# A two-layer decoder on one core: where the 16x16 inverses of the second self-attention run, and what stands between them

## The reference, cut to what matters

```python
A = jnp.tril(jnp.einsum('bhik,bhjk->bhij', K, K) * bt[:, :, None, :], -1)
Vn = jax.scipy.linalg.solve_triangular(eye + A, rhs, lower=True)   # rhs = V
scores = jnp.einsum('bqhd,bkhd->bhqk', q, k) * scale               # k times beta, causal mask
attn = jax.nn.softmax(scores, axis=-1)
out = jnp.einsum('bhqk,bkhd->bqhd', attn, v)                       # v is Vn
```

## Time and profile before

| what | us |
|---|---|
| median of three runs | 1125.17 (1124.74 to 1133.2) |
| the profiled execution, its own time | 1135.51 |
| its span, first to last instruction | 1133.7 |
| TensorE busy in the span | 989.1 |
| VectorE busy | 567.4 |
| ScalarE busy | 366.7 |
| GpSimd busy | 195.9 |

### The profile page before, as it was taken

One profiled execution on the slowest core, in us unless ns is written; L12 is line 12 of the kernel. 1 busy time (PEld: TensorE's weight loads), 2 busy tenths in 40 slices (PEclk: granted clock), 3 DMA queues, 4 the chain that ended last, 5 costly groups with the idle time before them and its releaser, 6 DMA issues.

```text
span 1133.7 us, 18852 instructions
## 1 busy us (share of the span) xinstructions
PE 989.1 (87%) x7392; PEld 619.5 (55%) x7392; DVE 567.4 (50%) x1153; ACT 366.7 (32%) x733; POOL 195.9 (17%) x233
## 2 busy tenths in 40 slices
PE   7998779998899999975863999889489999999994
PEld 4764423333468899962352568668345444444442
DVE  3789878885431111115687676356652333233325
ACT  4434436666222233322374453233221000000000
POOL 6000000000012222210036631060000111111110
PEclk9889869999799999986986999997679999999998
DMA  6000000000744555532001102030104022222001
GB/s 227 2 1 1 1 1 2 1 1 1 270 152 162 162 181 181 182 94 74 1 2 37 38 2 94 1 134 2 47 1 114 15 85 85 82 77 79 17 1 37
DMA packets 27209, 75.06 MB, mean 66 GB/s; under 512 B 9828, under 2 KB 17260, under 8 KB 21748
## 3 DMA queue, kind: packets, MB, share of 16 engines
q1 hardware_dynamic: 24916, 67.84, 18.1%
q0 software_dynamic: 2208, 6.03, 1.9%
HBM read 67.41 MB, written 6.46 MB: 65 GB/s over the span
## 4 chain that ended last, share of the span: by engine, by line
PE 71%; DVE 22%; issue 3%; ACT 2%; DMA 1%; POOL 0%; SPq 0%; DVEq 0%; ACTq 0%; POOLq 0%
PE psum L1519 8%; PE psum L1094 7%; PE psum L1106 7%; DVE arena L2073 4%; PE psum L1523 3%; PE psum L1285 3%; PE psum L1507 3%; PE psum L1549 2%; PE psum L1553 2%; PE psum L996 2%; PE psum L1485 2%; DVE arena L1996 2%; DVE arena L1997 2%; PE psum L1442 2%; PE psum L1255 1%
## 5 line engine op out<-in xcount | busy, mean ns | idle before, releaser
L1519 PE MATMUL psum<-arena 128*128 128x512 f32 (+1 forms) x192 | 92.0, 616 | 0.5 <-DVE arena L2500 0.5
L1950 ACT ACTIVATE arena<-psum 128x512 f32<-128x512 f32 (+1 forms) x32 | 19.0, 594 | 225.6 <-PE psum L1523 225.6
L2073 DVE TENSOR_REDUCE arena<-psum 128x2 f32<-128x512 f32 x128 | 82.7, 688 | 15.6 <-PE psum L942 13.4
L1770 ACT ACTIVATE arena<-psum,arena 128x128 f32<-128x128 f32 x184 | 52.6, 368 | 115.2 <-PE psum L1094 94.8
L1094 PE MATMUL psum<-arena 128*128 128x128 f32 x736 | 86.7, 276 | 0.0
L1094 PEld LDWEIGHTS psum<-arena 128*128 128x128 f32 x736 | 84.0, 192 | 2.7 <-issue 2.7
L736 POOL TENSOR_TENSOR arena<-arena 128x512 f32<-128x512 f32 (+1 forms) x32 | 40.5, 1265 | 254.6 <-ACT arena L1950 254.6
L1106 PE MATMUL psum<-arena 128*128 x368 | 83.1, 379 | 0.0
L2220 DVE COPY arena<-psum 128x256 f32<-128x256 f32 x23 | 9.8, 425 | 135.6 <-PE psum L1079 85.2
L1747 ACT ACTIVATE arena<-psum 128x1024 f32<-128x1024 f32 x64 | 65.5, 1025 | 33.9 <-PE psum L964 30.9
L1106 PEld LDWEIGHTS psum<-arena 128*128 128x128 f32 x368 | 68.2, 190 | 8.4
(11 more groups left out here) (354 smaller groups left out, 1867.8 us busy)
## 6 DMA issues: line engine op xcount, KB each, us to landing
arena<-in_w SPq DMA_DIRECT2D x31, 1024.0 KB, 13.4
arena<-in_experts SPq DMA_DIRECT2D x8, 1248.0 KB, 6.2
arena<-mixed SPq DMA_DIRECT2D x16, 256.0 KB
arena<-mixed SPq DMA_DIRECT2D x8, 512.0 KB
arena<-in_ctx SPq DMA_DIRECT2D x2, 1024.0 KB, 7.1
arena<-returned SPq DMA_DIRECT2D x8, 256.0 KB, 4.9
arena<-in_w_xattn SPq DMA_DIRECT2D x1, 1538.5 KB, 9.9
arena<-in_w_ffn SPq DMA_DIRECT2D x1, 1152.0 KB, 5.2
```

Source lines behind the costliest of these rows:

```text
L1519: pe.matmul(out, e[w][:, k, :], xe6[:, half, k, :], start=(k == 0), stop=False)
L1770: last = act.activation(hidt[:, r % 2, ic * P:(ic + 1) * P], bank(n)[:, i * P:(i + 1) * P], ACT.Gelu, bias=b1_tile[:, r % 4, ic:ic + 1])
L2073: ax_max.by(dve.tensor_reduce(nmx[:, b % 2, :, h], bank(u % 2).rearrange("p (t s) -> p t s", t=2), AX.X, ALU.max, negate=True))
```

## The change

- GpSimd inverts half 0, VectorE half 1. GpSimd's inverse is followed by `keys_by_head` for w = 3 and 4, then the unit copy, then w = 5 and later.
- The diagonal of half 0 is transposed within the loop of the key products: at j = 6, after the transposes of tile 6 and before the products of m = 5 (`DIAG_AFTER` = 4). Its four banks take places 20 to 23 in the turn of six banks, so later products move by four places (`slot1`, `before_slot`). ScalarE's four copies (`keep_diagonal(0)`) stand at the same place.
- For that, the gathers of half 0 come earlier: VectorE's two after the products of m = 3 at j = 5, and ScalarE's one becomes a GpSimd copy (`gather_pool`). `ti1` is blanked by halves, with 1 + 4 memsets each.
- VectorE waits for all eight diagonal copies, and inverts columns 0 to 3, 4 to 7, 8 to 11 and 12 to 14 with one softmax behind each group. `scores1(0)` no longer waits for the diagonal copies; the first rest product does.
- ScalarE's unit copies are cut in halves (`own_unit`) and set after the exponentials of w = 0 and 1, and into rounds t = 0 and 1 of the solve loop.
- `pt1` is used from its middle on (`probs1`), so that the first eight probabilities do not lie over `nd1` and `ti1`; the four buffers of `nd1` and `ti1` are split so that each can be written when the part of `qk1` under it has been read. SyncE's fetch of half 0 waits for half 0's transposes only.

```diff
@@ build: arena
 arena.at = first1_at
-nd1, ti1 = arena.take(2, CH, CHUNKS * CH), arena.take(2, CH, CHUNKS * CH)
+nd1_first, ti1_first, ti1_last, nd1_last = (arena.take(CH, CHUNKS * CH) for _ in range(4))
+nd1, ti1 = (nd1_first, nd1_last), (ti1_first, ti1_last)
...
@@ build: slots, invert1
 
-def invert1(engine, do, step, g):
-    less, inv = (v[:, g, :, :].rearrange("p j (c i) -> p j c i", c=CHUNKS) for v in (nd1, ti1))
-    for j in range(CH - 1):
+DIAG_AFTER = 4
+DIAG_SLOT = (4 * (DIAG_AFTER + 1), 4 * (NT + 1))
+
+def slot1(m, r):
+    return 4 * m + r + (CHUNKS if m > DIAG_AFTER else 0)
+
+def probs1(w):
+    return pt1[:, (w + NT) % (2 * NT), :]
+
+def invert1(engine, do, step, g, columns):
+    less, inv = (v[g].rearrange("p j (c i) -> p j c i", c=CHUNKS) for v in (nd1, ti1))
+    for j in columns:
...
@@ SyncE
 sp.wait_ge(ti1_ready[g].sem, 1)
-sp.dma_start(mine, ti1[:, g, :, :].rearrange("p j x -> p (j x)")).then_inc(ti1_out[g].sem, 16)
+sp.dma_start(mine, ti1[g].rearrange("p j x -> p (j x)")).then_inc(ti1_out[g].sem, 16)
...
 if g == 0:
-    sp.wait_ge(nd1_ps.sem, nd1_ps.base + 2 * CHUNKS)
+    sp.wait_ge(nd1_ps.sem, nd1_ps.base + CHUNKS)
...
@@ GpSimd
     keys_by_head(w)
-pool.wait_ge(tr1_ps.sem, 2 * NT)
-do(pool.memset(ti1.rearrange("p g j x -> p (g j x)"), 0.0))
-for m in range(CH):
-    pool.memset(ti1.rearrange("p g j (c i) -> p g j c i", c=CHUNKS)[:, :, m, :, m], 1.0)
+
+def unit_inverse(g):
+    flat = ti1[g].rearrange("p j x -> p (j x)")
+    do(pool.memset(flat, 0.0))
+    for c4 in range(CHUNKS):
+        pool.memset(flat[:, CH * c4:CH * c4 + (CH - 1) * (CHUNKS * CH + 1) + 1:CHUNKS * CH + 1], 1.0)
+
+pool.wait_ge(na_act.sem, na_act.base + 2 * 4)
+pool.wait_ge(na_dve.sem, na_dve.base + 2 * 4)
+pool.wait_ge(kb1_ready.sem, 3)
+do(pool.tensor_copy(na1[64:96, 0, 0:CH, :], na1[64:96, 2, 0:CH, :]), gather_pool)
+pool.wait_ge(tr1_ps.sem, 2 * 4)
+unit_inverse(0)
+pool.wait_ge(tr1_ps.sem, 2 * 6)
+unit_inverse(1)
...
                     c["ident"].rearrange("p (c w) -> p c w", c=CHUNKS)[:, :, 0:CH]), ti1_blank)
-pool.wait_ge(nd1_sb.sem, nd1_sb.base + 2 * CHUNKS)
-invert1(pool, do, pool_step, 1)
+pool.wait_ge(nd1_sb.sem, nd1_sb.base + CHUNKS)
+invert1(pool, do, pool_step, 0, range(CH - 1))
+for w in range(3, 5):
+    keys_by_head(w)
+pool.wait_ge(kb1_ready.sem, 5)
...
                     wide(c["ident"][96:P, 96:96 + CH], 1, B * KC * 8)), unit_pool)
-for w in range(3, 2 * NT):
+for w in range(5, 2 * NT):
...
@@ TensorE: before_slot, keys_by_keys
 
+def before_slot(n):
+    last = n - 6
+    if last < 0:
+        return
+    if DIAG_SLOT[0] <= last < DIAG_SLOT[0] + CHUNKS:
+        pe.wait_ge(nd1_sb.sem, nd1_sb.base + last - DIAG_SLOT[0] + 1)
+        return
+    m, r = divmod(last - (CHUNKS if last >= DIAG_SLOT[0] else 0), 4)
+    if r < 2:
+        pe.wait_ge(na_act.sem, na_act.base + 2 * m + r + 1)
+    else:
+        pe.wait_ge(na_dve.sem, na_dve.base + 2 * m + r - 1)
+
...
     for r in range(4):
-        n = 4 * m + r
-        if n >= 6:
-            m0, r0 = divmod(n - 6, 4)
-            if r0 < 2:
-                pe.wait_ge(na_act.sem, na_act.base + 2 * m0 + r0 + 1)
-            else:
-                pe.wait_ge(na_dve.sem, na_dve.base + 2 * m0 + r0 - 1)
+        before_slot(slot1(m, r))
...
             last = pe.matmul(
-                bank((4 * m + r) % 6).rearrange("p (c u e i) -> p c u e i", c=CHUNKS, u=4, e=2)[:, :, u, :, :],
+                bank(slot1(m, r) % 6).rearrange("p (c u e i) -> p c u e i", c=CHUNKS, u=4, e=2)[:, :, u, :, :],
...
@@ TensorE: turn_diagonal
 if g == 0:
-    pe.wait_ge(na_act.sem, na_act.base + 2 * NT)
-    pe.wait_ge(na_dve.sem, na_dve.base + 2 * NT)
-pe.wait_ge(gather_act.sem, gather_act.base + g + 1)
+    pe.wait_ge(gather_pool.sem, gather_pool.base + 1)
+else:
+    pe.wait_ge(gather_act.sem, gather_act.base + 1)
...
 for i in range(CH):
-    last = pe.transpose(bank(4 * g + i // 4)[:, (i % 4) * P:(i % 4 + 1) * P],
+    if i % 4 == 0:
+        before_slot(DIAG_SLOT[g] + i // 4)
+    last = pe.transpose(bank((DIAG_SLOT[g] + i // 4) % 6)[:, (i % 4) * P:(i % 4 + 1) * P],
...
@@ TensorE: the loop over tiles, scores1
         turn_heads1(j)
+    if j == DIAG_AFTER + 2:
+        turn_diagonal(0)
...
         keys_by_keys(j - 1)
-for g in range(2):
-    turn_diagonal(g)
+turn_diagonal(1)
...
         pe.wait_ge(causal_ready.sem, causal_ready.base + 1)
-        pe.wait_ge(nd1_sb.sem, nd1_sb.base + 2 * CHUNKS)
...
@@ TensorE: rest_of_chunk
 chunk, group = divmod(t, GROUPS)
+if t == 0:
+    pe.wait_ge(nd1_sb.sem, nd1_sb.base + 2 * CHUNKS)
...
     if chunk < 3:
-        pe.wait_ge(unit_act.sem, unit_act.base + chunk)
+        pe.wait_ge(unit_act.sem, unit_act.base + 2 * chunk)
...
@@ ScalarE: keep_products, gather
             na1[:, :, 4 * m:4 * m + 4, 32 * r:32 * r + 32],
-            bank((4 * m + r) % 6).rearrange("p (c u x) -> p c u x", c=CHUNKS, u=4), ACT.Copy))
-
-def gather(g):
-    act.wait_ge(na_act.sem, na_act.base + 2 * 4 * (g + 1))
-    act.wait_ge(na_dve.sem, na_dve.base + 2 * 4 * (g + 1))
-    gather_act.by(act.activation(na1[64:96, 0, g * CH:(g + 1) * CH, :], na1[64:96, 2, g * CH:(g + 1) * CH, :],
-                                 ACT.Copy))
+            bank(slot1(m, r) % 6).rearrange("p (c u x) -> p c u x", c=CHUNKS, u=4), ACT.Copy))
+
+def keep_diagonal(g):
+    for ib in range(CHUNKS):
+        act.wait_ge(nd1_ps.sem, nd1_ps.base + CHUNKS * g + ib + 1)
+        nd1_sb.by(act.activation(
+            nd1[g].rearrange("p j (c i) -> p i c j", c=CHUNKS)[:, 4 * ib:4 * ib + 4, :, :],
+            bank((DIAG_SLOT[g] + ib) % 6).rearrange("p (i c j) -> p i c j", i=4, c=CHUNKS)[:, :, :, 0:CH],
+            ACT.Copy))
...
@@ ScalarE: the loop over tiles
         ft_sb.by(last)
+    if j == DIAG_AFTER + 2:
+        keep_diagonal(0)
...
         keep_products(j - 1)
-    if j == NT - 1:
-        gather(0)
-gather(1)
-for n in range(2 * CHUNKS):
-    g, ib = divmod(n, CHUNKS)
-    act.wait_ge(nd1_ps.sem, nd1_ps.base + n + 1)
-    nd1_sb.by(act.activation(
-        nd1[:, g, :, :].rearrange("p j (c i) -> p i c j", c=CHUNKS)[:, 4 * ib:4 * ib + 4, :, :],
-        bank(n).rearrange("p (i c j) -> p i c j", i=4, c=CHUNKS)[:, :, :, 0:CH], ACT.Copy))
-for chunk in (1, 2):
+act.wait_ge(na_act.sem, na_act.base + 2 * NT)
+act.wait_ge(na_dve.sem, na_dve.base + 2 * NT)
+gather_act.by(act.activation(na1[64:96, 0, CH:2 * CH, :], na1[64:96, 2, CH:2 * CH, :], ACT.Copy))
+keep_diagonal(1)
+
+def own_unit(chunk, g):
...
         act.wait_ge(gather_dve.sem, gather_dve.base + 4)
+    elif g == 0:
+        act.wait_ge(gather_pool.sem, gather_pool.base + 1)
     else:
-        act.wait_ge(gather_act.sem, gather_act.base + 2)
+        act.wait_ge(gather_act.sem, gather_act.base + 1)
     rows = slice(32 * chunk, 32 * chunk + 32)
-    unit_act.by(act.activation(na1[rows, chunk, :, :].rearrange("p u (h i) -> p (u h) i", i=CH),
-                               wide(c["ident"][rows, 32 * chunk:32 * chunk + CH], 1, B * KC * 8), ACT.Copy))
+    unit_act.by(act.activation(na1[rows, chunk, g * CH:(g + 1) * CH, :].rearrange("p u (h i) -> p (u h) i", i=CH),
+                               wide(c["ident"][rows, 32 * chunk:32 * chunk + CH], 1, CH * 8), ACT.Copy))
...
@@ ScalarE: keep_probs
 act.wait_ge(pt_ps.sem, w + 1)
-if w == EARLY_W - 1:
+if w == NT:
...
         act.wait_ge(ti1_out[g].sem, 16)
-pt_sb.by(act.activation(pt1[:, w, :], bank(7), ACT.Copy))
+pt_sb.by(act.activation(probs1(w), bank(7), ACT.Copy))
...
@@ ScalarE: the loop of the solve
     keep_probs(w - 1)
+if w < 2:
+    own_unit(1, w)
...
     keep_probs(w - 1)
+if t < 2:
+    own_unit(2, t)
...
@@ VectorE: the loop over tiles
         keep_last_products(j - 2)
-gather(0)
+    if j == 5:
+        gather(0)
...
 gather(1)
-
-dve.wait_ge(ti1_blank.sem, ti1_blank.base + 1)
-dve.wait_ge(nd1_sb.sem, nd1_sb.base + CHUNKS)
-invert1(dve, do, dve_step, 0)
...
@@ VectorE: softmaxes and inverses
 
-for w in range(EARLY_W):
+dve.wait_ge(ti1_blank.sem, ti1_blank.base + 1)
+dve.wait_ge(nd1_sb.sem, nd1_sb.base + 2 * CHUNKS)
+for w in range(EARLY_W - 1):
+    invert1(dve, do, dve_step, 1, range(4 * w, 4 * w + 4))
     softmax1(w)
+invert1(dve, do, dve_step, 1, range(4 * EARLY_W - 4, CH - 1))
+softmax1(EARLY_W - 1)
...
```

More of the change, by code:

```diff
@@ L378, in build @@
         unit_pool = again("unit_pool", p_sub, 1)
+        gather_pool = again("gather_pool", b1_spread, 1)
         rest_ps = again("rest_ps", wct_ps, 2)
@@ L1342, in values1 @@
                         last = pe.matmul(bank(j % 2)[64 * p:64 * p + 64, at:at + 34],
-                                         pt1[:, 2 * j + q // 4, (q % 4) * P + 64 * p:(q % 4) * P + 64 * p + 64],
+                                         probs1(2 * j + q // 4)[:, (q % 4) * P + 64 * p:(q % 4) * P + 64 * p + 64],
                                          vb1[:, 2 * j + p, q, :], start=True, stop=True)
@@ L2274, in keep_last_products @@
                     na_dve.by(dve.tensor_copy(na1[:, :, 4 * m:4 * m + 4, 32 * r:32 * r + 32],
```

(2 more changed lines are left out.)

## The result

The changed kernel took 1145.45 us (median of four, 1139.85 to 1150.54), the kernel before 1129.18 over its four runs; the ratio is 1.0134 with a 95% interval of 1.0092 to 1.0176. The change makes the kernel 13 to 15 us slower. The forecast was 4 us slower, and the range ended at 1135, so the result lies outside it. The ratios leave out runs that stand apart at a longer time: two of the ten of b_best, one of the twelve of b_fill2 (2381.84), and two of the four of a_fill, for which none is given.

A forecast was written before the change was run, and what follows sets the result against it. TensorE's solve loop bounds; only its start moves. VectorE's inverse 7.7 us later, 8.5 of disturbances and 5.65 from softmax 2 put scores 4 at 635.4 against 631.42, +4.0 us: 1139.5 profiled, 1129 median, range 1116 to 1135.

The forecast's parts named there:

- What bounds the kernel: Second self-attention: TensorE's solve loop bounds (busy 62.77 of 64.60 us), so the change can only move the loop's start.
- Part 1, key products: Key products and early gathers: this part 5.2 us longer, VectorE's inverse starting at 607.3, 7.7 us later.
- Part 2, disturbances: VectorE's inverse with softmaxes between: GpSimd's work beside it adds 8.5 us, so softmax 2 ends at 629.6.
- 9.4 + 4.35: VectorE undisturbed: 24 inverse instructions of columns 0 to 11 with gaps 9.4 us, three softmaxes 4.35 us.
- the straight line: VectorE inverse instructions alone: durations interpolated between 0.22 us (60 elements) and 0.42 us (a 128x256 product).
- From softmax 2 to scores 4: TensorE's scores 3, transposes 2 and first rest product: 5.65 us, between 4.0 at full and 7.3 at half clock.
- in the loop nothing changes: Solve loop: ScalarE's unit copies fit beside rounds of 4.45 us and the second inverse arrives in time; no time added.
- rival C: Half clock reaches into the solve loop, some 3.8 us more a round; two rounds give 1137; chance 0.05.
- Rival A: VectorE runs its columns at its own pace, the port not binding: 4.7 to 8 us faster, 1119; chance 0.22.
- Rival B: Key products hide the first half, VectorE's inverse starts at 599.6 undisturbed: 12 us faster, 1113; chance 0.05.
- What would show it: Signs: gathers over 3.5 us, tile 6 near 589, an inverse instruction over 3, VectorE's first near 607, scores 4 near 635.
- The base: Kernel before: median 1125.17 us, to which the +4.0 us from the profiled execution was carried, giving 1129.

The follow-up runs named there:

- b_best: Kernel before with softmaxes between VectorE's columns, keys_by_head between GpSimd's, unit copy behind keys_by_head(7), 11 and 15 unread matmuls behind scores 1 and 2: ratio 0.9984.
- b_fill2: Kernel before with unread matmuls added on TensorE, 68 behind scores 0 and 2 behind each of the next two: ratio 1.0001.
- a_fill: Changed kernel with 14, 18 and 3 unread matmuls added between the early scores on TensorE: no ratio given, loop 68.0 us.
- a_gact: Changed kernel with the third early gather of half 0 on ScalarE instead of GpSimd: ratio to before 1.0089.
- a_unitlate: Changed kernel with GpSimd's 32x4096 unit copy moved behind keys_by_head(7): ratio to before 1.0061.
- a_fill2: Changed kernel with 29, 40 and 19 unread matmuls between the early scores, leaving TensorE gaps of 0.7 us at most: ratio to before 1.0023.
- a_late_fill: Changed kernel with the unit copy behind keys_by_head(7) and 29, 26 and 15 unread matmuls between the early scores: ratio to before 1.0001.
- b_split: Kernel before with only the softmaxes set between VectorE's columns and keys_by_head 3 and 4 ahead of the unit copy (with probs1): ratio 0.997.
- a_again: Changed kernel unedited, run once more for a second profiled execution: ratio to before 1.0118.

## Why the prediction was wrong

- *What bounds the kernel.* Right in what the loop waits for: the mask matmul's wait for the softmax is still TensorE's longest in the stretch ahead of it. Wrong in its conclusion that the change can only move the moment at which the loop starts: of the 15.9 us the start has 7.1, and the loop itself grew by 8.8.
- *Part 1, key products.* Right in path and size. The key products are 5.3 us longer, forecast 5.2; VectorE's inverse starts 8.1 later (39.5 against 31.4), forecast 7.7. The diagonal transposes of half 0 took 3.52, forecast 3.0. The early gathers took 4.05, forecast 4.3, but the reason given for it holds in part only: without the GpSimd copy they took 3.19 (a_gact), not 2.5.
- *Part 2, disturbances.* From VectorE's first inverse instruction to the end of softmax 2 it took 610.55 to 633.97, 23.4 us, against 9.4 + 4.35 = 13.75 undisturbed: 9.7, forecast 8.5. By the instructions' durations against the straight line, the first eight lost 2.4 (forecast 2.6) and those beside `keys_by_head(3)` and `(4)` 3.1 (3.2). The unit copy cost 3.3 (a_unitlate), forecast 2.7 between 0 and 3.6, and `keys_by_head(5)` 0.7, which the forecast named but left out of its sum.
- *From softmax 2 to scores 4.* Forecast 5.65 between 4.0 and 7.3; measured 7.2 (634.11 to 641.29), the whole at half clock. Scores 4 thus start 7.1 us later than before, forecast 4.0; the forecast's own range ended at 7.4.
- **The step that failed** is the sentence that in the loop nothing changes, with rival C at a chance of 0.05: the term for the loop was put at 0 and measured 8.8 us. C was the right rival, with its price of 3.8 us a round and two rounds or more (3.3, 3.7 and 1.7 us measured in three rounds, all of the 8.8). It was set low because the loop keeps TensorE busy without a gap, and because the clock had come back within 4 us from 595.21 and within 8 from 619.15. Neither carried over: it took 26.4 us from 634.1. I took the speed of its return from two stretches of other work as if it were a constant, where the one execution shown gave no more than two samples, neither with a rest product in it. That the loss in the loop goes with the clock is shown (a_fill2: 62.8 with the clock at 1.00); why the clock returned so late is not.
- *Rival A* (the port does not bind) is refuted by the 3.70 us instruction and its 0.42 without the copy. *Rival B* is refuted by VectorE's first inverse instruction at 39.5, not 31.4. Of these 8.1 us, 5.3 come from the first half's gathers and transposes, which hold up tile 6 and all behind it, and 2.8 from VectorE now waiting for the second half's gather and transposes. They eat what hiding half of the inverses gives: even without the unit copy and with the clock at 1.00 the change gains nothing (a_late_fill).
- *What would show it.* The signs were named, and on the scale of the kernel before (2.8 us less) they came: gathers over 3.5 us, tile 6 near 589 (588.8), an inverse instruction over 3 us, VectorE's first one near 607 (607.7), and a clock of 0.5 past 640 for C. Scores 4 came at 638.5, not near 635.
- *The base.* The forecast of 1129 was made from a median of 1125.17 over three runs; the four runs beside the changed kernel have 1129.18. So 4 of the 16 us between forecast and result are the base's scatter, and 12 the kernel's. Moved by these 4 us the range would have ended at 1139, still 6 short of the result.

Of the 15.9 us of the stage, 8.1 come with the later inverse, 8.8 with the half clock in the loop, and 1.0 is won between the inverse's start and scores 4.

## What to carry to other kernels

When work is spread so that a fine-grained alternation of two engines feeds TensorE a little at a time, price the clock at which the next dense stretch starts, and take the half-clock case as a full rival, not as a tail: here it cost 8.8 us in one kernel, and nothing in b_split. Before moving work to an idle GpSimd, list every VectorE instruction beside it with two SBUF inputs: part of the gain is paid back there, and one GpSimd copy of 3.67 us cost VectorE 3.3. Work put earlier into a chain of three engines that hand over tile by tile (key products here) is on the path even if every engine has slack on average: the early gathers delayed one VectorE multiplication by 4.1 us, and with the transposes behind them the whole chain by 5.3.

## What the runs showed of the hardware

- The granted clock can stay at 1.2 GHz for 26.5 us while TensorE is busy 26.39 of them (the third stretch of the changed kernel); in a_again and a_gact it came back at the same distance from the stage's start (89.7, against 89.5). In b_split it rose 3.4 us after the last gap. From scores 1 on, all twelve rises outside fill in the fourteen profiles came within 0.4 us of the end of a group of transposes.
- 88 matmuls whose result nobody reads, 19.5 us of work in TensorE's idle time, made the stage 11.3 us shorter (a_fill2).
- One VectorE instruction of 252 elements took 3.70 us beside a GpSimd copy of 3.67, and 0.42 without it.
